# Gate projections of the first eight units in earlier ticks, through DRAM, and five steps of the pipeline in another order

## What is computed

```python
mixed = hidden_states @ w_qkv                      # 256 -> 8192
z = (hidden_states @ w_z).reshape(B, S, HV, DV)    # 256 -> 32 heads x 128
...
mixed = jax.nn.silu(y).transpose(0, 2, 1)          # y: causal convolution of 4 taps along the tokens
q, k, v = jnp.split(mixed, [KEY_DIM, 2 * KEY_DIM], axis=-1)
...
q = _l2norm(q) * DK ** (-0.5)
k = _l2norm(k)
def step(Sm, inp):
    Sm = Sm * jnp.exp(g_)[..., None, None]
    kv = jnp.einsum('bhk,bhkv->bhv', k_, Sm)
    delta = (v_ - kv) * b_[..., None]
    Sm = Sm + jnp.einsum('bhk,bhv->bhkv', k_, delta)
    o = jnp.einsum('bhk,bhkv->bhv', q_, Sm)
...
og = o * jax.nn.silu(z)
var = jnp.mean(og * og, axis=-1, keepdims=True)
on = og * jax.lax.rsqrt(var + EPS) * norm_w
return on.reshape(B, S, VAL_DIM) @ w_out
```

## Time and profile before

| | us |
|---|---|
| median of three executions | 2258.57 |
| lowest and highest | 2254.74, 2260.4 |
| the profiled execution, its own time | 2255.11 |
| its span | 2253.2 |
| PE busy in the span | 2091.6 (93%) |
| DVE busy | 1711.3 (76%) |
| ACT busy | 1512.7 (67%) |
| POOL busy | 904.1 (40%) |

### The profile page before, as it was taken

The page is one execution under the profiler, slowest core; times in us unless marked ns, Lnnn a source line. Parts: engine busy times, 40 slices in busy tenths (PEclk is TensorE's granted clock), DMA queues, the critical chain, the costliest instruction groups (busy, mean ns, idle before and its releaser), DMA issues.

```text
span 2253.2 us, 49295 instructions
## 1 busy us (share of the span) xinstructions
PE 2091.6 (93%) x18636; PEld 1716.1 (76%) x18636; DVE 1711.3 (76%) x2944; ACT 1512.7 (67%) x3585; POOL 904.1 (40%) x714
## 2 busy tenths in 40 slices
PE   4659999999999999999999999999988899999998
PEld 4448888888888888888888888887776476666776
DVE  6789797887879788787977978787325777767665
ACT  4547777777777777777777677775767666565632
POOL 1534454444445445445535534532333123213232
PEclk8779999999999999999999999998999999999999
DMA  3432322322232332233233222212243012322232
GB/s 77 94 73 48 89 44 72 63 64 67 55 85 46 72 75 49 68 60 80 52 70 72 48 70 56 75 34 56 58 137 133 1 66 76 104 94 73 91 136 85
DMA packets 274633, 161.56 MB, mean 72 GB/s; under 512 B 209352, under 2 KB 246752, under 8 KB 269280
## 3 DMA queue, kind: packets, MB, share of 16 engines
q1 hardware_dynamic: 274400, 158.41, 27.6%
HBM read 122.43 MB, written 35.91 MB: 70 GB/s over the span
## 4 chain that ended last, share of the span: by engine, by line
issue 36%; POOL 26%; PE 23%; DVE 8%; ACT 4%; DMA 2%; SPq 2%; POOLq 0%; DVEq 0%; ACTq 0%
POOL SM L577 5%; POOL EB L493 5%; POOL Q L555 5%; PE ps L1739 4%; POOL SZ L579 3%; PE ps L1347 3%; POOL EB L497 3%; PE ps L1349 3%; PE ps L1348 3%; POOL WL L471 2%; POOL SM L585 2%; PE ps L1660 1%; ACT SC L856 1%; PE ps L1651 1%; PE ps L1480 1%
## 5 line engine op out<-in xcount | busy, mean ns | idle before, releaser
L909 DVE SCALAR_TENSOR_TENSOR A<-ps,CW,A 128x508 f32<-128x508 f32 (+2 forms) x768 | 515.9, 734 | 55.3 <-ACT A L671 50.1
L572 POOL TENSOR_SCALAR SM<-SM 128x8 f32<-128x8 f32 x64 | 12.6, 196 | 813.8 <-ACT DL L690 813.8
L1480 PE MATMUL ps<-WO,DL 128*128 128x256 f32 x1008 | 244.5, 394 | 39.5 <-POOL WO L484 24.5
L1480 PEld LDWEIGHTS ps<-WO,DL 128*128 128x128 f32 x1008 | 189.7, 194 | 74.5 <-POOL WO L484 26.4
L1347 PE MATMUL ps<-XH,WH 128*128 128x512 f32 x512 | 221.5, 433 | 26.7 <-DVE A L909 25.8
L1127 DVE TENSOR_TENSOR SZ<-SZ,ps 128x512 f32<-128x512 f32 x128 | 87.7, 687 | 201.5 <-PE ps L1514 201.4
L1349 PE MATMUL ps<-XH,WL 128*128 128x512 f32 x512 | 206.4, 403 | 0.0
L1348 PE MATMUL ps<-XL,WH 128*128 128x512 f32 x512 | 205.2, 401 | 0.0
L690 ACT ACTIVATE DL<-SZ 128x128 f32<-128x128 f32 x512 | 152.4, 298 | 38.5 <-PE ps L1514 28.8
L856 ACT ACTIVATE SC<-ps,A 128x128 f32<-128x128 f32 x512 | 141.7, 386 | 51.5 <-DVE A L1252 50.7
L1112 DVE TENSOR_TENSOR BP<-ps,EB 128x512 f32<-128x512 f32 x256 | 158.3, 681 | 3.3 <-ACT EB L665 3.3
(11 more groups left out here) (225 smaller groups left out, 5556.1 us busy)
## 6 DMA issues: line engine op xcount, KB each, us to landing
EB<-decay_rows SPq DMA_DIRECT2D x128, 256.0 KB, 4.7
WE<-expert_halves SPq DMA_DIRECT2D x32, 1024.0 KB, 5.1
x_blocks<-BP SPq DMA_DIRECT2D x256, 32.0 KB, 1.7
X<-x_blocks SPq DMA_DIRECT2D x16, 512.0 KB, 6.5
tt_blocks<-TI SPq DMA_DIRECT2D x16, 512.0 KB, 2.6
tn_blocks<-TM SPq DMA_DIRECT2D x16, 512.0 KB, 2.6
TTF<-tt_blocks SPq DMA_DIRECT2D x256, 32.0 KB, 1.9
expert_halves<-BP SPq DMA_DIRECT2D x8, 1024.0 KB, 5.8
```

The lines of the kernel that those rows point to most:

```text
L909: dve.scalar_tensor_tensor(acc, ps(i, 0, [[128, 4], [1, 128 - s]]), at(CW, tile * 4 + 3 - s, [[1, 1]]), acc, ALU.mult, ALU.add).then_inc(s ...
L1480: t = pe.matmul(ps(7 - i, b * 256, [[1, 256]]), at(on_buf(k), (4 * i + 2 * b + v) * 128, [[1, 128]]), at(WO, v * 256, [[1, 256]]), start=( ...
```

## The change

- **z of units 0 to 7** (`NZ = 8`). Their projections are made in ticks 4 to 7, two units in each, behind `kq_mm`, in banks 4 and 5 for even and 6 and 7 for odd units. ACT applies SiLU behind the decay exponentials of the tick, SP stores the 512 KB of each unit in DRAM (`first_gates`) at the end of its tick, and loads them back in ticks 8 to 15, near the head of the tick (`load_gates`), once `on_tr` of unit m - 2 has freed the buffer. The gates of these units wait for the load. In ticks 8 to 15 PE has no z projection and ACT no `z_silu`. The weights of z for the first two pairs are loaded and split earlier (splits in ticks 3 and 6, on ACT and POOL).
- **v transposes** stand behind the outputs for units m = 0 to 6; for all others ahead of them, as before.
- **Output weights.** `load_wo` is issued at the end of SP's tick with k % 4 == 3, not at the head of the next. In the middle this is the same place in the queue but for the tick's number; in the last units (tick 68) it comes to stand ahead of the experts' and the context's loads. POOL scales them ahead of the normalising chain of that tick, not behind the squares Q of the next one. The power for the key norms goes ahead of the chain too.
- **Copies on ACT.** `tn` stands behind `on_T` (both halves) and `tt128`, not between the two halves of `on_T`.
- **Taps on DVE.** The first two taps of unit n + 1 both stand ahead of the two gates. Before, the first stood behind the gates and the second at the head of the next tick, where the third remains. Of the room for the inverse (4060 + 2000 in a tick) 5260 now stand ahead of the v taps and 800 ahead of the q and k taps.
- Two semaphores of the setup are merged into another; nothing is reordered by it.

```diff
@@ SP
+                def store_z(m):
+                    sp.wait_ge(sem["z_silu"], 2 * m + 2)
...
+                    sp.dma_start(z_scr[m], at(SZ, (m % 2) * 1024, full)).then_inc(sem["st_z"], 16)
+                def load_gates(m):
+                    if m >= 2:
+                        sp.wait_ge(sem["on_tr"], 2 * (m - 2) + 2)
...
+                    sp.dma_start(at(SZ, (m % 2) * 1024, full), z_scr[m]).then_inc(sem["ld_zb"], 16)
@@ SP, for n in range(NT)
-                    if 0 < k < NSTEP and k % 4 == 0:
-                        load_wo(k // 4)
                     if n % 4 == 0 and 4 <= n <= NSTEP:
                         load_x(n // 4 - 1)
-                    if 0 <= m < NSTEP and m % 4 == 1 and m // 4 + 1 < HK:
+                    if n == 4:
+                        load_z(1)
+                    if 4 <= m < NSTEP and m % 4 == 1 and m // 4 + 1 < HK:
                         load_z(m // 4 + 1)
+                    if 0 <= m < NZ:
+                        load_gates(m)
...
                     if n + 3 < NSTEP:
                         load_rows(n + 3)
+                    if 0 <= k and k % 4 == 3 and k + 1 < NSTEP:
+                        load_wo(k // 4 + 1)
+                    if 4 <= n < 4 + NZ // 2:
+                        store_z(2 * n - 8)
+                        store_z(2 * n - 7)
@@ POOL, for n in range(NT)
-                    if 0 < k < NSTEP and k % 4 == 0:
-                        scale_wo(k // 4)
                     if EARLY - 1 <= n and n + 2 < NSTEP:
                         decay(n + 2)
+                    if n in (3, 6):
+                        split_lo("z", W_Z, n // 3 - 1)
...
+                    if n % 4 == 0 and 4 <= n <= NSTEP:
...
+                                           at(SM, C_PH, [[0, 4], [1, 4]]), ALU.pow).then_inc(sem["sk"], 1)
+                    if 0 <= k and k % 4 == 3 and k + 1 < NSTEP:
+                        scale_wo(k // 4 + 1)
@@ ACT, for n in range(NT)
-                    if s3:
+                    if s3 and m >= NZ:
                         z_silu(m, 0)
-                    if s3:
                         z_silu(m, 1)
...
+                    if 4 <= n < 4 + NZ // 2:
+                        for m0 in (2 * n - 8, 2 * n - 7):
+                            z_silu(m0, 0)
+                            z_silu(m0, 1)
                     if s4 and k < NSTEP - 1:
                         on_T(k, 0)
+                    if s4 and k < NSTEP - 1:
+                        on_T(k, 1)
+                    if s3:
+                        act.wait_ge(sem["tt128"], m + 1)
...
                     if sv and vn % 4 == 0:
                         act.wait_ge(sem["inv"], INV_OPS * (vn // 4 + 1))
...
@@ DVE
                 def gate(m, i):
-                    dve.wait_ge(sem["z_silu"], 2 * m + 1 + i)
+                    if m >= NZ:
+                        dve.wait_ge(sem["z_silu"], 2 * m + 1 + i)
+                    else:
+                        dve.wait_ge(sem["ld_zb"], 16 * (m + 1))
@@ DVE, for n in range(NT)
-                    if s1 and (n > EARLY or n == 0):
+                    if s1 and n == 0:
                         kq_tap(n, 2)
...
-                    pump(2500)
-                    pump(1560)
+                    if s1:
+                        pump(5260)
...
-                    pump(2000)
+                    if s1:
+                        pump(800)
+                    else:
+                        pump(2000)
+                    if EARLY <= n and n + 1 < NSTEP:
+                        kq_tap(n + 1, 1)
+                        kq_tap(n + 1, 2)
                     if s3:
                         gate(m, 0)
...
-                    if EARLY <= n and n + 1 < NSTEP:
-                        kq_tap(n + 1, 1)
@@ PE
                 def on_tr(k, i):
                     if i == 0:
                         pe.wait_ge(sem["on"], k + 1)
-                    if k + 1 < NSTEP:
+                    if k + 1 < NZ:
+                        pe.wait_ge(sem["vv"], 4 * (k + 1) + 2 + 2 * i)
+                    elif k + 1 < NSTEP:
                         pe.wait_ge(sem["z_silu"], 2 * (k + 1) + 1 + i)
@@ PE, for n in range(NT)
-                    if s3:
+                    if s3 and m >= NZ:
                         z_proj(m, 0)
...
+                    if 4 <= n < 4 + NZ // 2:
+                        for m0 in (2 * n - 8, 2 * n - 7):
+                            z_proj(m0, 0)
+                            z_proj(m0, 1)
...
+                    if sv and not 0 <= m < NZ - 1:
+                        v_trs(vn, m)
                     if s3:
                         outputs(m, 0)
...
+                    if 0 <= m < NZ - 1:
+                        v_trs(vn, m)
```

89 lines of the change are left out of this document (54 added, 35 removed).

## The result

| kernel | median us | ratio to before, 95% interval | gates of unit 0 | eight ticks from there | mean group of four ticks, units 8 to 48 |
|---|---|---|---|---|---|
| before | 2256.65 | | 178.5 | 194.4 | 97.9 |
| changed | 2289.05 | 1.0142 [1.0127, 1.0157] | 186.5 | 206.4 | 99.9 |

The profiled execution of the changed kernel took 2291.2 us, its span 2289.3. The last units (48 to 63) took 355.0 against 357.3. In the two traces the spans differ by 36.1: 8.0 up to the gates of unit 0, 12.0 in the next eight ticks, 19.8 in the forty behind them, -2.3 in the last units and -1.3 behind them.

What follows compares the result with a forecast made beforehand. PE was taken to bound the steady ticks (busy 959.21 of 978.70 us), DVE to set the end in tick 5. Terms -2.5 - 5.4 - 4.8 - 6.5 = -19.2 gave 2238 us, range 2222 to 2250.

Steps and rivals of the forecast that it cites:

- steady groups: Groups of four ticks, units 8 to 55: WO, `tt128`, gates and inverse together give -0.4 by twelve, -4.8 us.
- the inverse's rooms: Steady groups: more inverse ahead of the v taps makes them net 0.1 to 1.3 late, 1.2 given back: 0.
- ticks 9 to 15: Ticks without z: PE drops 3.2 us in each, part of it comes through: -5.4 us together.
- z in ticks 4 to 7: Early z projections fit PE's idle time, not quite free; with tick 8's gain, -2.5 us for ticks 4 to 8.
- the second does: Ticks 9 to 15: dropping z's second half lets L1546 start earlier, some 1.0 us per tick, seven times -7.0.
- WO in the middle: Steady groups: WO is scaled ahead of the chain, which just fits; PE's wait goes, -1.3 us per group.
- `tt128`: Steady groups: the 0.6 us copy wait goes, but PE then waits for delta: -0.1 to -0.6.
- Gates: Steady groups: gates later behind the taps, 0.14 us in three ticks, 0.6 in the copy's tick: +1.0.
- The last units: Last WO issued some 13 us sooner: -5.6, 1.8 of PE's 7.4 wait staying; `tt128` wait -0.9; together -6.5 us.
- Rival 4's second half: POOL's chain and the inverse stretch each other, 0.4 us a tick after slack, +22, 2260; chance 0.04.
- rival 2: Taps ahead of the gates make L1533 wait, 0.6 us in each of 55 ticks, +33, 2271; chance 0.07.

Runs made afterwards that it cites:

- pump_before: The changed kernel with only the rooms for the inverse as before (2500 + 1560 ahead of the v taps, 2000 behind `y_add`): 2264.21 us.
- wo_only: The kernel before with WO's load at the end of SyncE's tick, and its scaling and the key norms' power ahead of GpSimd's chain: 2266.68 us.
- z_only: The kernel before with only z of units 0 to 7 made in ticks 4 to 7 through DRAM, and v transposes behind outputs for units 0 to 6: 2263.14 us.
- z_vtr: z_only with the v transposes ahead of the outputs, as before, and no z matmuls in ticks 8 to 15: 2257.48 us.
- z_fill: z_vtr with 24 z matmuls, whose results nobody reads, put back in each of ticks 8 to 15: 2255.07 us.
- wo_early: The kernel before with WO loaded between SyncE's two block loads and scaled ahead of GpSimd's chain, the power staying behind the chain: 2231.66 us.
- act_only: The kernel before with only ScalarE's `tn` copy moved behind both `on_T` and `tt128`: 2250.25 us.
- pump_only: The kernel before with only the rooms for the inverse changed, to 5260 ahead of the v taps and 800 behind `y_add`: 2353.27 us.
- taps_before: The changed kernel with only the taps as before (first behind the gates, second at the head of the next tick): 2370.59 us.

## Why the prediction was wrong

The step that failed at the highest price is in the steady groups: "Net 0.1 to 1.3 late, of which the room ahead of the next gates, now 800 instead of 2000 ns, gives 1.2 back: 0", the term of the inverse's rooms. It measured +97 us alone, and 25 in the changed kernel (pump_before). A second failed in ticks 9 to 15, where -5.4 became +12.0. The steady groups together were to give -0.4 each and cost 2.0. The parts, in the order of the prediction:

**z in ticks 4 to 7, -2.5 predicted.** PE's idle time did take the projections. But the gates of unit 0 can't be read from the changed kernel alone: in its profiled execution, and in those of wo_only and z_only, the setup ahead of tick 0 ran at the lower clock, and the first q and k projection starts at 27.5 to 27.8 instead of 22.7 to 23.4 in all the others, kernels with and without z moved. In those others the gates of unit 0 have a median of 178.3 with z moved (seven kernels) and 179.3 without (eight): -1.0, within their spread of 175 to 183. The setup of the changed kernel:

```profile
22.00:24.00 2.00, 2.00 (x11) 2.00 (x11) 1.13 (x2) 1.22 (x2) 0.00 (x0) 0.50 0.04 8
```

The same of the kernel before:

```profile
22.00:24.00 2.00, 2.00 (x18) 1.91 (x18) 0.38 (x3) 0.14 (x1) 0.00 (x0) 1.00 0.00 0
```

Not foreseen was that z waits itself: 8.7 us in tick 6 of the changed kernel, for the low parts of z's second weights, which POOL makes behind the decays. What this costs no run separates.

**Ticks 9 to 15, -5.4 predicted.** The step that failed is "the second does": I let PE's dropped work pass through up to the next wait, at unchanged speed. Measured +9.5 for z alone (z_only, 203.9 against 194.4; 7.7 in z_vtr), +12.0 in all. Behind the idle time that the early z leaves, the clock falls to its lower level for some microseconds; with that time filled (z_fill) the ticks take 194.4, as before. I had the trace's own sign of it: 0.60 and PE busy 7.81 of 22.00 in the earlier trace rows.

**WO in the middle, -1.3 per group predicted.** PE's wait went. The chain ended in time for `on_tr` in most groups, as worked out: in wo_only four of ten wait for it, 0.7 at most, in the changed kernel three, 1.0 at most. What I left out was that the chain, 2 us later, lies beside the two large products of the inverse. wo_only lost 0.7 per group; wo_early, which leaves the chain in place, gained 1.4.

**`tt128`, -0.1: right.** act_only shows the wait again at delta.

**Gates, +1.0 per group predicted.** The term is mis-sized, by the tick with WO: 0.67 for 0.14, in all 1.5, and 1.9 with the long ones. The late gates were sized rightly in the three other ticks. What I left out is that the moved taps move the inverse too, onto POOL's chain: the power there takes 0.46 more, WO is scaled later and PE's wait for it grows from 1.3 to 1.9; in two of ten ticks the clock falls behind it.

**The inverse's rooms, 0 predicted.** This is the step with the price: 97 us alone, 25 between pump_before and the changed kernel. I counted instructions and slack (0.1 to 1.3 late) at the durations of before. They don't keep them once they run beside POOL. The sentence from the Trainium skill (SBUF — State Buffer, Who interferes with whom) described it; the runs agree: 0.69 becomes up to 2.4 where the products start while one of POOL's that reads is running, and stays 0.69 where they don't. I priced it at 0.4 a tick with a chance of 4 in 100; in pump_only the groups are 1.7 a tick longer, with the added instructions ahead of the v taps and the clock in it.

**The last units, -6.5 predicted.** Right in mechanism: PE's idle time ahead of the products with the last WO was 7.41 and is 2.78 in wo_only, 2.72 in the changed kernel, where I had left 1.8, and the copy's 0.9 goes in act_only. The length of the stretch fell by 5.6 in wo_only and by 2.3 in the changed kernel, but kernels with the same order there differ by 5, so this term's size isn't confirmed.

Rival 4's second half had the mechanism, at 2260; rival 2's 2271 came nearest in number, by a cause that taps_before rules out as the main one: with the taps back behind the gates the kernel is slower still. Both had too little of the chance, and neither was combined with the other.
